# Attention tiles handled in pairs: a changed instruction order in an 8-core attention and feed-forward kernel

## What is computed

```python
def _L0_attn_ref(x, w_qkv, w_proj, b_proj):            # H = 16 heads of 64
    q, k, v = ...                                      # from x @ w_qkv.T
    scores = jnp.einsum('bhqd,bhkd->bhqk', q, k) * hs ** (-0.5)
    p = jax.nn.softplus(scores)
    p = p * p
    p = p * causal
    attn = p / (jnp.sum(p, axis=-1, keepdims=True) + 1e-09)
    out = jnp.einsum('bhqk,bhkd->bhqd', attn, v)
    return jnp.einsum('btc,oc->bto', out, w_proj) + b_proj

# _L0_ffn_ref: h = qat_lora_linear(x, W_fc, ...); h = gelu(h); qat_lora_linear(h, W_proj, ...)
# qat_lora_linear: 8-bit fake quantised weight (scale = max|W| / 127), plus 2 * (x A^T) B^T, rank 16

x = _layernorm(x + attn(x));  x = _layernorm(x + ffn(x))
```

## Time and profile before

| | |
|---|---|
| median of 3 runs | 2143.85 us (2142.18 to 2145.31) |
| the profiled execution | 2140.47 us |
| its span, slowest core | 2138.9 us |
| spans of the 8 cores | 2126.6 to 2138.9 us |
| TensorE busy | 1929.6 us (90% of the span) |
| VectorE busy | 1042.4 us (49%) |
| ScalarE busy | 855.0 us (40%) |
| GpSimd busy | 448.2 us (21%) |

### The profile page before, as it was taken

One profiled execution on the slowest core, in us unless ns is written; L12 is line 12 of the kernel. 1 busy time (PEld: TensorE's weight loads), 2 busy tenths in 40 slices (PEclk: granted clock), 3 DMA queues, 4 the chain that ended last, 5 costly groups with the idle time before them and its releaser, 6 DMA issues.

```text
span 2138.9 us, 26841 instructions; the slowest of 8 cores (2126.6 to 2138.9 us)
## 1 busy us (share of the span) xinstructions
PE 1929.6 (90%) x8834; PEld 759.0 (35%) x8834; DVE 1042.4 (49%) x1613; ACT 855.0 (40%) x1026; POOL 448.2 (21%) x515
## 2 busy tenths in 40 slices
PE   6897987888987899999867889999999999999998
PEld 2332332222322333322222234444444444444443
DVE  2675887766689777788759731111110101020202
ACT  2464765765422466677533421212222121313130
POOL 1121221221156412222225421111010101010201
PEclk9998998999999999999978999999999999999999
DMA  8656554357466443344485465020202111110101
GB/s 130 149 135 146 155 150 131 100 128 149 122 188 181 131 112 116 114 124 128 125 222 163 133 191 169 30 69 30 70 30 59 40 50 50 50 60 20 60 10 49
DMA packets 118023, 228.35 MB, mean 107 GB/s; under 512 B 59282, under 2 KB 59538, under 8 KB 115186
## 3 DMA queue, kind: packets, MB, share of 16 engines
q1 hardware_dynamic: 109042, 195.03, 30.2%
q0 software_dynamic: 8848, 31.63, 8.7%
HBM read 182.21 MB, written 58.98 MB: 113 GB/s over the span
## 4 chain that ended last, share of the span: by engine, by line
PE 72%; DVE 10%; DMA 8%; issue 6%; POOL 2%; ACT 2%; SPq 0%; DVEq 0%; POOLq 0%; ACTq 0%
PE ps_s L924 20%; PE ps_a L976 10%; PE ps_f L976 10%; PE ps_a L718 8%; PE ps_f L341 8%; PE ps_s L674 6%; PE ps_f L365 5%; DVE a_ph L700 3%; DMA a_bc<-recscr 3%; PE ps_f L616 3%; DVE a_QO L776 2%; DMA recscr<-g_rec 2%; PE ps_f L497 2%; DMA g_den<-a_nd 1%; ACT a_ph L685 1%
## 5 line engine op out<-in xcount | busy, mean ns | idle before, releaser
L685 ACT ACTIVATE a_ph<-ps_s 128x1024 bf16<-128x1024 f32 (+1 forms) x576 | 560.7, 976 | 506.8 <-PE ps_s L674 505.4
L931 ACT ACTIVATE b_h<-ps_s,g_bfc,g_scl 128x512 bf16<-128x512 f32 x256 | 199.1, 778 | 649.1 <-PE ps_s L924 649.1
L924 PE MATMUL ps_s<-b_xT,b_Wfc 128*128 128x512 bf16 x2048 | 444.0, 379 | 0.0
L718 PE MATMUL ps_a<-a_ph,a_V 128*65 128x512 bf16 (+3 forms) x1280 | 354.0, 366 | 94.4 <-DVE a_ph L700 73.5
L700 DVE TENSOR_TENSOR a_ph<-a_ph 128x1024 bf16<-128x1024 bf16 (+1 forms) x576 | 399.9, 719 | 24.9 <-ACT a_ph L685 12.8
L341 PE MATMUL ps_f<-a_xT,a_wqk 128*128 128x512 bf16 x1024 | 307.5, 396 | 35.5 <-DMA a_xT<-xT 16.9
L692 POOL TENSOR_TENSOR a_ph<-a_ph,g_mask 128x256 bf16<-128x256 bf16 x256 | 196.4, 785 | 498.6 <-ACT a_ph L685 497.7
L981 DVE SCALAR_TENSOR_TENSOR g_x<-ps_a,g_scl,g_x 128x512 f32<-128x512 f32 x32 | 24.0, 751 | 566.1 <-PE ps_a L976 566.1
L924 PEld LDWEIGHTS ps_s<-b_xT,b_Wfc 128*128 128x128 bf16 x2048 | 200.4, 98 | 241.6 <-issue 0.2
L674 PE MATMUL ps_s<-a_QO,a_K 64*128 64x512 bf16 (+3 forms) x1280 | 226.3, 367 | 2.6 <-ACT a_QO L351 2.5
L976 PE MATMUL ps_a<-b_Wp,b_h 128*128 128x512 bf16 x1024 | 224.4, 379 | 0.0
(11 more groups left out here) (47 smaller groups left out, 937.1 us busy)
## 6 DMA issues: line engine op xcount, KB each, us to landing
a_w<-wfc SPq DMA_DIRECT2D x64, 512.0 KB, 5.7
a_w<-wpF SPq DMA_DIRECT2D x64, 512.0 KB, 4.5
a_bc<-recscr SPq DMA_DIRECT2D x64, 256.0 KB, 4.4
g_x<-x SPq DMA_DIRECT2D x32, 512.0 KB, 4.0
x1scr<-g_x SPq DMA_DIRECT2D x32, 512.0 KB, 4.0
g_x<-x1scr SPq DMA_DIRECT2D x32, 512.0 KB, 3.2
out<-g_x SPq DMA_DIRECT2D x32, 512.0 KB, 2.6
a_wqk<-wqk POOLq DMA_DIRECT2D x16, 512.0 KB, 7.4
```

Source lines behind the costliest of these rows:

```text
L685: s_read[sl] = P.op("scalar", lambda E: E.activation(dst, src, AF.Softplus, scale=HS ** -0.5), waits=[tok, ph_av[q]])
L718: tok = P.op("tensor", lambda E, c0=c0, n=n, off=off, x0=x0, hd=hd, fin=fin: E.matmul(ps_a[0:65, hd * 512 + c0: hd * 512 + c0 + n], V4[:, ...
L924: tok = P.op("tensor", lambda E, cc=cc, c0=c0: E.matmul(ps, b_Wfc[:, c0:c0 + 128], b_xT[:, (g % 2) * 4096 + cc * 512:(g % 2) * 4096 + (cc ...
L931: h_tok[(g, f)] = P.op("scalar", lambda E: E.activation(b_h[:, f * 512:(f + 1) * 512], ps, AF.Gelu, bias=g_bfc[:, f:f + 1], scale=g_scl[:, ...
```

## The change

The loop handles two units in an iteration: the scores of both stand together, then the fillers of both, then the AV matmuls of the two units before. A merge matmul now stands right behind the scores. VectorE's evacuations of V chains and merges are held back and recorded behind the next squares. Where the older of the two closes a group, its AV comes ahead of the fillers.

```diff
+        for u in range(0, NU + 2, 2):
...
                 emit_scores(u)
-            if 2 <= u <= NU + 1:
+                emit_scores(u + 1)
+                cols = u_cols(u) + u_cols(u + 1)
+                merge_some(1.2 - (cols_left - cols) / cols_all)
+            if u >= 2:
                 emit_square(u - 2)
+                run_due()
+                emit_square(u - 1)
+            else:
+                run_due()
+            evacuate()
             run_due()
+            split = u >= 2 and seq_units[u - 2][4]
+            if split:
+                emit_av(u - 2)
             if u < NU:
-                left = sum(c.left for c in chains) + mg["want"] - mg["took"]
-                carry = pump(carry + left * u_cols(u) / cols_left)
-                cols_left -= u_cols(u)
-            if u >= 3:
-                emit_av(u - 3)
+                left = sum(c.left for c in chains)
+                carry = pump(carry + left * cols / cols_left)
+                cols_left -= cols
+            if u >= 2:
+                if not split:
+                    emit_av(u - 2)
+                emit_av(u - 1)
```

Holding back (`held`, `evacuate`); `ch_v` and the add of `merge_half` go through it:

```diff
+        def evacuate(bank=None):
+
+            while held and (bank is None or any(b == bank for b, _ in held)):
+                held.pop(0)[1]()
 
         def take_bank():
             i = bank_i[0] % 2
+            evacuate(i)
...
+        def merge_some(part):
+
+            if not chains or mg["took"] >= min(mg["want"], mg["want"] * part):
+                return
+            c = chains[0]
+            late = mg["want"] * part - mg["took"] >= 2
+            if c.key[0] in ("qk", "v") and (late or 1 <= c.done <= 6):
                 mg["took"] += 1
                 merge_half(mg["done"])
                 mg["done"] += 1
...
-            mg["want"] = {5: 10, 6: 10, 7: 24, 9: 14, 10: 14, 11: 14, 12: 14, 13: 14, 14: 14}.get(gp, 0)
+            mg["want"] = {5: 15, 6: 15, 7: 18, 9: 16, 10: 16, 11: 16, 12: 16, 13: 16}.get(gp, 0)
```

AV of the second head takes 128 columns of V (the first head's last 63, its ones, and its own 64), so that its result lies on partitions 64 to 127 and its denominator on 63; the broadcast buffer is split into two of 512 columns, both heads' halves side by side on the partitions:

```diff
+                    if hd == 0:
+                        lhs, rows = a_V[:, x0:x0 + 65], 65
+                    else:
+                        lhs, rows = a_V[:, x0 + 1:x0 + 129], 128
...
-            def turn():
-                bc_turn.append(spread_out)
-                if len(bc_turn) == 1:
-                    spread_out()
-
             def spread_out():
-                st["d4"] = P.dma("sync", msem("bc"), lambda E: E.dma_start(
-                    out=a_bc[0:64, :], in_=d_rec[b:b + 1, :].broadcast_to([64, 1024])),
-                    waits=[st["d3"], bc_free[0]])
-                after_ticks(3, scale)
+                for hd in range(2):
+                    st[2 + hd] = P.dma("sync", msem(f"bc{hd}{b}"), lambda E, hd=hd: E.dma_start(
+                        out=a_bc[hd * 64:hd * 64 + 64, b * 512:(b + 1) * 512],
+                        in_=d_rec[b:b + 1, hd * 512:(hd + 1) * 512].broadcast_to([64, 512])),
+                        waits=[st["d3"], bc_free[b]])
...
-            after_ticks(1, fetch)
-            after_ticks(4, recip)
-            after_ticks(5, put)
-            after_ticks(7, turn)
+            after_ticks(2, fetch)
+            after_ticks(5, recip)
+            after_ticks(6, put)
+            after_ticks(8, spread_out)
+            after_ticks(11, scale)
```

`fetch` is two DMAs too. The first layer norm's last step goes from VectorE to ScalarE, with one more small GpSimd step (mean times factor):

```diff
+            if n < NT:
+                ta = P.op("scalar", lambda E: E.activation(
+                    x, x, AF.Identity, bias=g_mv[:, q * 4 + 2:q * 4 + 3],
+                    scale=g_mv[:, q * 4 + 3:q * 4 + 4]), waits=[ln_wait.pop(n)])
+            else:
+                ta = P.op("vector", lambda E: E.tensor_scalar(
+                    x, x, g_mv[:, q * 4:q * 4 + 1], g_mv[:, q * 4 + 3:q * 4 + 4],
+                    ALU.subtract, ALU.mult), waits=[ln_wait.pop(n)])
```

The weight tiles of `do_absmax` go through six slots (three of a_w, three of g_x), and a load is recorded only once its slot's reader has been:

```diff
+        def w_slot(k):
+
+            return k % 6 if k < 64 else k % 3
...
         def w_take(k):
-            for i in range(k, k + 2):
-                w_load(i)
-            after_ticks(2, lambda: w_load(k + 2))
-            return (k % 3) * 1024
+            w_fill(k)
+            after_ticks(4, w_fill)
+            return w_tile(k)
```

206 lines of the change are left out of this document (120 added, 86 removed).

## The result

The changed kernel took **2211.1 us** (median of 4 runs, 2207.9 to 2384.2) where the kernel before took 2143.0 on the same chip: 1.031 times as long, interval 1.0292 to 1.0329. The prediction was 2029, with a range from 1980 to 2115. It is wrong in sign and by 182 us; only rival C stands on the right side, and it stops at 2181. Some executions of any kernel here run at a lower granted clock on one half of the chip and take longer; a ratio leaves them out and a median does not, so where the two disagree, read the ratio.

The account below looks back on a forecast made before the run. TensorE was near its own pace only in pairs 9 to 13; elsewhere in-order VectorE, sometimes blocked by late DMAs, set the pace. Terms summed to -115 from 2140.5, 2025.5, plus 3.4 to the median: 2029 us, range 1980 to 2115.

Parts of the forecast that it names:

- rival C: Whole kernel slower: AV right behind its squares waits for them, 152 us, 2181 in all; chance 0.10.
- Norm chain: nothing: Denominators, reciprocals and broadcasts: smaller, doubled pieces still fit the six ticks, 0 us; bounds minus 20 to plus 30.
- the five gains of 19 to 27 us: Pairs 9 to 13 -19 us, 5 to 7 -27, 1 to 4 -26, pair 8 -27, 14 and 15 -26.
- Pairs of scores, -58 us on TensorE: Attention loop: 288 entries into scores instead of 576, at 0.20 us each, 58 us less for TensorE.
- Merge behind the scores, -13 us: Three changes of array shape instead of two times two, 128 x 0.10 = 13 us less for TensorE.
- I take 280 where 250/0.91 would be 275: Pairs 9 to 13: TensorE and VectorE both need 250 us, so 280 us instead of 299.2, minus 19.
- Rival B: Order-bound waits for late DMAs stay, so only 34 us less, 2110 us; chance 0.19.
- Rival D: The granted clock comes back too as waits shorten, and copies cost nothing: 2029 - 45 = 1984 us; chance 0.10.
- Pairs 1 to 4, -26 us: Weight slots and broadcast buffers remove VectorE's waits, VectorE at 84%: 237 us for 262.7; from 0 to minus 45.
- VectorE without the layer norm: Pair 8: last step moves to ScalarE at 0.98 us, VectorE falls from 114 to 82, stretch to 109 us, minus 27.
- nothing there changes: Feed-forward part, from 1267.1 us on: full clock, TensorE busy 862 of 872 us, no change in time.
- The copy behind a pair, +16 us: ScalarE's copy for 32 groups stands behind two softplus and delays AV 0.5 us each, plus 16; bounds 0 and 45.

Follow-up runs that it names:

- The pairing alone: The kernel before with only the loop over two units, merges inside the chains and nothing held back: 1.006.
- the bundle: Two broadcast buffers and fetches, six weight slots, 128-row AV, halved first load, later stores and norm chain, added to the pairing with the projection part: 1.0195.
- six slots: The change with six softplus slots for four, AV two units later, two weight slots for merges: 1.0422; the same with 256-byte pieces: 1.011.
- the pairing with the projection part: The kernel before with the two-unit loop, layer norm's last step on ScalarE behind the second half and x loaded between the halves: 1.0027.

## Why the prediction was wrong, point by point

Two steps failed. The forecast missed by 182 us, and the small pieces, the term "Norm chain: nothing", are 38 of them. The larger failure is the step from what the engines need to the time, the five gains of 19 to 27 us by shares of busy time: with 32-byte pieces the change is still some 29 us slower than before, where the sum had it 115 faster.

- **"Norm chain: nothing" failed.** It was to stand by 1.7 us or 3.4 us for the put, because six ticks left 9.3 us for a chain of 6.9 or 8.6. The put did go to 3.0 us, near the doubling I had written down, and by medians the chain still fits: 0.33 + 3.0 + 0.5 + 4.7 = 8.5. Two things were wrong with "nothing". The median is not the price: the chain's slack is used up by the late ones, and VectorE's waits went from 16 to 24 with 36.5 us more. And a small transfer is not alone: a_bc and other stores beside it got slower too, in the kernel before by 1.1 us for a_bc and 1.7 us for wpb. Measured, this term is +38 us in the change, +69 in it with the merges in the chains and +96 in the kernel before, against an upper bound of +30. I named the Trainium skill's rule against it (DMA: Bandwidth & Descriptors, Specifications), that transfers under 512 bytes are read, modified and written, and put it aside. As a warning it was right. But by it pieces of 32 and of 256 bytes should suffer too, and the runs show a step between 16 and 32 and nothing from there to 256; here the measurement decides. Whether a read and a second write are behind it no run shows, nor whether the doubled count or the halved size does it.
- **Pairs of scores, -58 us on TensorE: right as a mechanism.** Four score matmuls of two units take 0.61 us in this row, 0.39 + 0.22, so the second unit follows at full pace:

```profile
888.05 0.61 PE L741 MATMUL ps_s<-a_QO,a_K 64*128 64x512 bf16 x4
...
888.59 0.39 PE L546 MATMUL ps_f<-a_lo,a_lo 16*128 16x512 bf16 x1
...
888.91 1.47 PE L367 MATMUL ps_f<-a_xT,a_wqk 128*128 128x512 bf16 x6
```

  Up to the last group TensorE is busy 958.5 us for 1004.1, of which a part is records missing from the trace (4494 matmuls for 4572, with 4565 weight loads for 4568). What failed is the step after it, that the time follows TensorE's need. The pairing alone, with this saving, is 13 us *slower*.
- **Merge behind the scores, -13 us: right as a price.** In the rows above the scores' second pair starts at 888.27, the merge 0.32 us later and the filler 0.32 after that. Where no merge stands between, a filler starts 0.31 us after the scores. So a merge costs 0.32 us here, and 0.42 in a chain, where it has 0.32 on each side in place of one 0.22 (medians of starts in both traces): 0.10 less, 128 times. The time did not follow this either.
- **"I take 280 where 250/0.91 would be 275", the shares of busy time: the larger failure.** I took the leading engine's share from the old order, or raised it: 89% after 91 in pairs 9 to 13, 83 after 79 in 5 to 7, 84 after 76 in 1 to 4, 87 after 84 in pair 8. They are the outcome of an order, not a property of the engine. In pairs 9 to 13 VectorE's 250 us were forecast to the microsecond, and the wall came out at 341.2 instead of 280, a share of 73%. As I read it, two engines of nearly equal load that hand over to each other in every iteration need slack, and the change took slack away, in the lead (83 us by itself) and in the two banks that fillers, adds and copies share (91.6 us of waits in the stretches that lose). Taking one wait away mostly moved it to the next, so no run shows one of them as the cause, and what in the bundle takes another 36 us stays open.
- **Rival C, given 0.10, had the direction and a part of the mechanism.** Its 152 us for the shorter lead stood against gains that did not come either, so that its 2181 lies near the result partly by luck. The lead costs 83 us when nothing pays for it and 13 net when the pairing does. My argument against it, that VectorE can run ahead since squares wait only for an older softplus, was wrong because VectorE is in order: scalings, adds and V copies that wait for DMA or TensorE stand between it and the squares. Its own marker, over 100 us of AV waits, came true at 112.9 us. But most of these waits lie outside the stretches that lose, and where they were cured, with six slots, the time did not fall clearly: they are one link of the chain and not the whole loss.
- **Rival B's marker came true as well**: waits for a_bc and g_den did not shrink, they grew by half. Two broadcast buffers removed the turn and not the lateness. Its price, 34 us less than before, had the wrong sign too.
- **Rival D's clock went the other way.** From 0.93 to 0.87 in pairs 5 to 7 and from 0.99 to 0.94 in pairs 9 to 13. By the two levels that is 64 and 41 us at the lower one, after 31 and 6. If TensorE set the pace in all of it, half of the difference, some 34 us, is the clock's share of the 68.7 (an estimate, and an upper one: the pairing alone loses 15 us in pairs 9 to 13 at 0.99). No run separates it. (The stretches outside pairs 9 to 13 are 968 us long, not the 800 of the prediction.)
- **Pairs 1 to 4, -26 us: came out +8.6.** Six weight slots did halve VectorE's waits for weight tiles, from 19.5 to 9.7 us. With 32-byte pieces the stretch took 248.7 us, 14 less than before (of which pair 0 gave back 12, 129.3 for 117.5), and the small pieces took back the rest.
- **VectorE without the layer norm: right for VectorE, mostly not for the time.** It is busy 87.88 us in pair 8 for 113.96. The step costs ScalarE 1.24 us and not the estimated 0.98:

```profile
L650 ACT ACTIVATE g_x<-g_x,g_mv 128x1024 f32<-128x1024 f32 x32 | 39.7, 1241 | 61.5 <-POOL g_mv L639 61.4
```

  But pair 8 fell by 2.6 us, not 27. In that stretch ScalarE waits 42.0 us for GpSimd's statistics, GpSimd 27.9 for x, and projection chains 26.8 for the residual add: the chain of one tile took VectorE's place as the bound. The stretch of 14 and 15 gave 16.9 of 26, with 14 merges moved away from it. And ScalarE's queue has the Gelus behind this step: that cost 8.6 us where the prediction had "nothing there changes".
- **The copy behind a pair, +16 us: too high.** AV waited 8.3 us for ScalarE's copy (16 times) and 1.2 for VectorE's, 9.5 in all, where VectorE's took 11.2 before.
- **Feed-forward, "nothing there changes": wrong by 8.2 us**, 880.0 for 871.8, for the reason just given.
- **The chances.** 0.87 for faster rested on five gains of 19 to 27 us that all used one assumption, that busy shares hold or rise. They were one bet, not five.

## What to carry to other kernels

Before changing the layout of a small side transfer, price its pieces and every DMA beside it: going from 32 to 16 bytes a piece, 4 KB at a time, cost 4.5% of one kernel and 1.8% of the other, of 228 MB moved on a core. When work is paired to save an entry into an engine, count how many operations of the in-order partner now stand between a producer and its consumer; the lead lost can cost more than the entry saved. And never carry a utilisation over from an old order to a new one: build the reordering and the DMA layout as separate versions, since each hides the size of the other. When a step moves to another engine, look at what stands behind it on the new queue when its input is late, not only at whether the engine has room.

## What the runs showed of the hardware that I had not expected

- Pieces of 16 bytes in 64 groups' denominators and reciprocals (17408 packets under 512 bytes more on a core) made the kernel before 4.5% slower (with one more fetch a group); pieces of 256 bytes instead of 32 made it no faster (1.004). The Trainium skill (DMA: Bandwidth & Descriptors, How a descriptor splits into AXI transactions) gives a beat of 32 bytes; the step lies where a piece no longer fills one. That the one comes from the other no run here shows.
- They slowed transfers that had not changed: the 256 KB broadcast from 4.4 to 5.5 us, a 256 KB store from 2.3 to 4.0 us, medians of 64 and 32.
- A layer norm step of 128x1024 float32 with scale and bias takes 1.24 us on ScalarE, and 2.12 on VectorE in pair 8. The same VectorE step takes 0.80 in the feed-forward part (mean of 32, the pairing with the projection part). What VectorE shares with others in pair 8, where GpSimd is busy 82 of 136 us, was not tried apart.
- The average granted clock of a stretch fell with short stops spread over it, without a long one: in pairs 9 to 13 from 0.99 to 0.94, where TensorE's longest stop was 2.7 us before and 3.4 in the change, and its stops of over 1 us add up to 12 and 40 us.
